# First token quad in four pieces of 32 times, and its fp32 products over nine chunks that stay in memory

## What is computed

```python
x = x + wkv(decay, bonus, layernorm(x), ctx)        # a recurrence over 128 times, per channel
x = x + ffn(layernorm(x), ...)                      # 16 x 128 tokens, D = 512

# wkv, one step: y = (p + E*v) / (q + E);  p, q = decayed p, q plus exp(k)*v, exp(k)
# ffn:
gates = softmax(xf @ gate_w + gate_b)               # top 2 of 16 experts
routed = sum over the 2 experts of gate * (gelu(xf @ ew1 + eb1) @ ew2 + eb2)     # 128 hidden
shared = sum over 2 experts of (gelu(xf @ sw1 + sb1) @ sw2 + sb2)                # 2048 hidden each
```

## Time and profile before

| | |
|---|---|
| Time, median of 3 runs | 881.39 us (880.78 to 884.62) |
| The profiled execution | 879.35 us, of it 877.7 us between its first and last instruction |
| TensorE busy | 844.0 us, 96% |
| VectorE, ScalarE, GpSimd busy | 637.5, 490.8, 185.4 us |
| First instruction of the first split product | 58.85 us |

### The profile page before, as it was taken

One profiled execution on the slowest core, in us unless ns is written; L12 is line 12 of the kernel. 1 busy time (PEld: TensorE's weight loads), 2 busy tenths in 40 slices (PEclk: granted clock), 3 DMA queues, 4 the chain that ended last, 5 costly groups with the idle time before them and its releaser, 6 DMA issues.

```text
span 877.7 us, 14872 instructions
## 1 busy us (share of the span) xinstructions
PE 844.0 (96%) x4054; PEld 700.4 (80%) x4054; DVE 637.5 (73%) x1339; ACT 490.8 (56%) x871; POOL 185.4 (21%) x223
## 2 busy tenths in 40 slices
PE   2599999999999999999999999999999999999997
PEld 2468888888888888888888888888888799897886
DVE  7977988766587778565777786555676698983973
ACT  7737666354476553454656463445455388885531
POOL 2100000121100000122000001110221577764850
PEclk9999999999999999999999999999999999999999
DMA  8353433377343333574433324565687378868985
GB/s 218 97 169 103 139 110 107 105 159 143 93 149 97 97 96 100 125 172 83 157 107 96 97 74 107 119 146 158 179 203 176 113 235 250 256 224 313 307 253 146
DMA packets 124592, 133.37 MB, mean 152 GB/s; under 512 B 10264, under 2 KB 86608, under 8 KB 124012
## 3 DMA queue, kind: packets, MB, share of 16 engines
q1 hardware_dynamic: 115180, 106.90, 44.7%
q0 software_dynamic: 8784, 25.11, 9.5%
q10 hardware_dynamic: 560, 0.55, 0.2%
HBM read 109.53 MB, written 22.98 MB: 151 GB/s over the span
## 4 chain that ended last, share of the span: by engine, by line
PE 94%; DVE 3%; issue 1%; POOL 1%; ACT 0%; DMA 0%; POOLq 0%; ACTq 0%; DVEq 0%
PE up L600 13%; PE up L602 13%; PE up L601 13%; PE acc L662 13%; PE acc L667 13%; PE acc L664 13%; PE up L854 2%; PE up L856 2%; PE acc L600 2%; PE up L763 1%; PE acc L602 1%; PE acc L601 1%; PE misc L627 1%; PE up L627 1%; PE acc L772 1%
## 5 line engine op out<-in xcount | busy, mean ns | idle before, releaser
L600 PE MATMUL up<-xs,w1hi 128*128 128x512 f32 (+1 forms) x512 | 200.9, 392 | 0.0
L602 PE MATMUL up<-xs,w1lo 128*128 128x512 f32 (+1 forms) x512 | 197.6, 386 | 0.0
L601 PE MATMUL up<-xs,w1hi 128*128 128x512 f32 (+1 forms) x512 | 197.2, 385 | 0.0
L662 PE MATMUL acc<-w2hi,hhi 128*128 128x512 f32 x494 | 192.7, 390 | 0.0
L664 PE MATMUL acc<-w2lo,hhi 128*128 128x512 f32 x494 | 192.3, 389 | 0.0
L925 ACT ACTIVATE hhi<-up,b_col 128x512 fp32r<-128x512 f32 x128 | 87.3, 682 | 157.1 <-PE up L602 124.8
L1181 DVE TENSOR_TENSOR hlo<-hf,hhi 128x512 fp32r<-128x512 f32 x128 | 86.8, 678 | 86.6 <-ACT hf L928 40.7
L667 PE MATMUL acc<-w2hi,hlo 128*128 128x512 f32 x494 | 132.6, 389 | 0.0
L602 PEld LDWEIGHTS up<-xs,w1lo 128*128 128x128 f32 x512 | 96.2, 188 | 20.0
L601 PEld LDWEIGHTS up<-xs,w1hi 128*128 128x128 f32 x512 | 96.3, 188 | 18.8 <-issue 0.2
L600 PEld LDWEIGHTS up<-xs,w1hi 128*128 128x128 f32 x512 | 96.2, 188 | 18.8 <-issue 0.2
(11 more groups left out here) (274 smaller groups left out, 1165.1 us busy)
## 6 DMA issues: line engine op xcount, KB each, us to landing
w_raw<-in_L_ffn_sw SPq DMA_DIRECT2D x266, 256.0 KB, 2.9
expert_rows<-ysb SPq DMA_DIRECT2D x47, 256.0 KB
xn_rows<-kn POOLq DMA_DIRECT2D x16, 256.0 KB, 8.0
e2raw<-in_L_ffn_ew SPq DMA_DIRECT2D x16, 256.0 KB, 5.1
ew_sb<-in_L_ffn_ew SPq DMA_DIRECT2D x16, 256.0 KB
X<-in_x SPq DMA_DIRECT2D x12, 256.0 KB, 8.9
vin<-in_ctx SPq DMA_DIRECT2D x12, 256.0 KB
out<-X SPq DMA_DIRECT2D x12, 256.0 KB, 3.9
```

The costliest lines, as they stand in the source:

```text
L600: nc.tensor.matmul(o, lhs[0], rhs[0], start=start, stop=False)
L601: nc.tensor.matmul(o, lhs[0], rhs[1], start=False, stop=False)
L602: return nc.tensor.matmul(o, lhs[1], rhs[0], start=False, stop=stop)
L662: nc.tensor.matmul(acc[t][:], hh, w2hi[:, slot], start=first and (q > 0 or t >= HT) or again, stop=False)
```

## The change

The first quad is worked on in four pieces of 32 times, one tile each, in place of two of 64; every step of the first stage is done per tile, with its own semaphore counts, and the state of the scans is carried over three joints. `PRE` goes from 5 to 9: nine chunks, kept in memory of their own for the whole stage (`pw_a`, `pw_b`, `pw_c`), are multiplied in fp32 for tile 0 and then for tile 1 (18 steps n, 128 tokens each), so that nine chunks of the main stage are done for half the tokens. The queues of the stage are written anew; part of the work on one table (`boost0`) goes from ScalarE to VectorE (`boost_args`); eight transfers of the values are issued by ScalarE. In the first quad's main stage the loop over tiles is written out. What is computed is the same.

```diff
-    PRE = 5
+    PRE = 9
+    N0 = (TB // 2) * PRE
+    T1 = TT + 1
...
-                for j in range(3):
-                    step(at + j)
-                    tile(0, j)
-            with eng.Fori(1 if q == 0 else 0, TB - 1) as tb:
-                for j in range(3):
-                    step(at + 3 * tb + j, at + j)
-                    tile(tb, j)
+                for tb in range(TB - 1):
+                    for j in range(3):
+                        step(at + 3 * tb + j)
+                        tile(tb, j)
+            else:
+                with eng.Fori(0, TB - 1) as tb:
+                    for j in range(3):
+                        step(at + 3 * tb + j, at + j)
...
+            load_tiles([0])
+            load_tiles([1])
+            load_tiles([2, 3])
+            load_values([2, 3])
+            load_pre(0)
+            load_pre(1)
...
-            for p in range(RING):
-                load_pre_w1(p)
-                load_pre_w2(p)
+            for p in range(2, PRE):
+                load_pre(p)
+            for c in range(RING):
+                load_w1(c, c, chunk_of(c))
+                load_w2(c, c, chunk_of(c))
             load_quad(1)
...
+            key_T(0)
+            value_T(0)
+            key_T(1)
+            for i in range(1, TB):
+                value_T(i)
...
-            for tb in range(HT, TB):
-                key_T(tb)
-            value_T(HT)
+            def pre_up_product(n):
+                i, p = divmod(n, PRE)
+                pe.wait_ge(pw1_in[p], 16)
+                pe.wait_ge(xf_ok, i + 1)
+                need(pe, pre_h, n - 2)
                 for k in range(KC):
-                    last = nc.tensor.matmul(up[slot][:, 0:HQ], w1_raw[:, slot, k],
-                                            xf[:, k], start=k == 0, stop=k == KC - 1)
+                    last = nc.tensor.matmul(up[n % RING][:, 0:P], early_w1(p)[:, P * k:P * k + P], xf[:, k, P * i:P * i + P],
+                                            start=k == 0, stop=k == KC - 1)
                 last.then_inc(pre_up, 1)
 
-            def pre_down_product(p):
-                slot = pre_slot(p)
-                pe.wait_ge(pw2_in[slot], 16 * (p // RING + 1))
-                pe.wait_ge(pre_h, p + 1)
-                for t in range(HT):
-                    last = nc.tensor.matmul(acc[t][:], hf[:, slot, P * t:P * t + P], w2_raw[:, slot],
-                                            start=p == 0, stop=False)
-                last.then_inc(pre_down, 1)
-
-            for tb in range(HT):
-                transpose_x(tb, xn[:, tb], acc[HT + tb])
-            pe.wait_ge(xf_ok, HT)
+            def pre_down_product(n):
+                i, p = divmod(n, PRE)
+                pe.wait_ge(pw2_in[p], 16)
+                pe.wait_ge(pre_h, n + 1)
+                nc.tensor.matmul(acc[i][:], hf[:, n % RING, piece(n)], early_w2(p), start=p == 0, stop=False)\
+                    .then_inc(pre_down, 1)
+
+            pe.wait_ge(ek_ok, HT)
+            pe.wait_ge(v_ok, HT + 1)
             pre_up_product(0)
             pre_up_product(1)
-            pe.wait_ge(wexp.sem, wexp.at(1, "e"))
-            pe.wait_ge(ek_half, 2)
-            for p in range(PRE):
-                if p + 2 < PRE:
-                    pre_up_product(p + 2)
-                if p == PRE - 2:
-                    for tb in range(HT, TB):
-                        transpose_x(tb, xn[:, tb], acc[tb])
-                if p == 1:
-                    for tb in range(HT, TB):
-                        result_T(tb)
-                pre_down_product(p)
+            for n in range(N0):
+                if n == 1:
+                    key_T(3)
+                if n in RESULT_AT:
+                    result_T(RESULT_AT[n])
+                if n in X_AT:
+                    early_x(X_AT[n])
+                if n + 2 < N0:
+                    pre_up_product(n + 2)
+                pre_down_product(n)
...
+            def early_reciprocal(i):
+                act.wait_ge(wkv0.sem, wkv0.at(i, "den"))
+                nc.scalar.activation(part(yy, i), part(den, i), ACT.Ln).then_inc(rec0.sem, 1)
+                act.wait_ge(rec0.sem, rec0.at(i, "ln"))
+                nc.scalar.activation(part(yy, i), part(yy, i), ACT.Exp, scale=-1.0).then_inc(rec0.sem, 1)
...
+            first_keep()
+            first_grow()
+            early_exp(0)
+            first_boost()
+            early_values(0)
+            early_exp(1)
+            early_values(1)
+            for b in range(CB // 2):
+                table_grow(b)
+            early_reciprocal(0)
+            for b in range(CB // 2, CB):
+                table_grow(b)
             act.wait_ge(b1_ps, 1)
             nc.scalar.copy(b1_col[:], misc[:, 0:CH]).then_inc(b1_ok, 1)
+            for i in range(HT, TB):
+                early_values(i)
+            for b in range(CB - 6):
+                table_relu(b)
+            x_full(0)
+            early_exp(2)
+            for n in range(2):
+                pre_gelu(n)
+            for b in range(CB - 6, CB):
+                table_relu(b)
+            early_reciprocal(1)
+            early_exp(3)
+            for n in range(2, 5):
+                pre_gelu(n)
+            x_full(1)
+            for n in range(5, 9):
+                pre_gelu(n)
+            x_hi_again(0)
+            early_reciprocal(2)
+            for n in range(9, 11):
+                pre_gelu(n)
+            x_hi_again(1)
+            pre_gelu(11)
+            act.wait_ge(c_in, 16 * 10)
+            for at in (0, 32, 64):
+                nc.scalar.copy(bias_r[at:at + 32], bias_f[at:at + 32]).then_inc(bias_hi, 1)
+            pre_gelu(12)
+            pre_gelu(13)
+            x_hi(2, 1, 2, x_bank[2])
+            pre_gelu(14)
+            early_reciprocal(3)
             table_boost()
+            for n in range(15, N0):
+                pre_gelu(n)
+                split_w1(n - 15, n - 15)
+            x_hi(3, 1, 3, x_bank[3])
 
...
+            def boost_args():
+                dve.wait_ge(pcon.sem, pcon.at(0, "ramp"))
+                after(tab, 0, "uw")
+                for b in range(KC):
+                    last = V.tensor_scalar(boost0[:, b, 1:], ramp[:, 1:], w_down[:, CB + b:CB + b + 1],
+                                           uw[:, CB + b:CB + b + 1], ALU.mult, ALU.add)
+                last.then_inc(boost_arg, 1)
+                dve.wait_ge(boost_arg, 1)
+                V.tensor_scalar(boost0[:, :, 1:], boost0[:, :, 1:], CAP, None, ALU.min).then_inc(boost_arg, 1)
...
+            early_ln1(0)
             tables()
-            early_ln1(0)
             early_ln1_apply(0)
             early_ln1(1)
+            boost_args()
+            early_ln1_apply(1)
             early_es(0)
             early_h(0)
             early_hv(0)
             early_den(0)
-            early_ln1_apply(1)
+            early_ev(0)
             early_num(0)
             early_result(0)
-            early_es(1)
+            early_ln1(2)
             early_add(0)
             early_ln2(0)
+            early_ln1_apply(2)
+            early_ln2_apply(0)
+            early_es(1)
             early_h(1)
-            early_ln2_apply(0)
             early_hv(1)
             early_den(1)
+            early_ln1(3)
+            early_ev(1)
+            early_ln1_apply(3)
             early_num(1)
             early_result(1)
-            for tb in range(HT):
-                x_lo_again(tb)
+            early_es(2)
             early_add(1)
             early_ln2(1)
+            early_h(2)
+            early_ln2_apply(1)
+            early_hv(2)
+            early_den(2)
+            early_ev(2)
+            early_num(2)
+            early_result(2)
+            early_es(3)
+            early_add(2)
+            early_ln2(2)
+            early_h(3)
+            early_ln2_apply(2)
+            early_hv(3)
+            early_den(3)
+            x_lo_again(0)
+            x_lo_again(1)
+            early_ev(3)
+            early_num(3)
+            x_lo(2, 1, 2, x_bank[2])
+            early_result(3)
             gate_weights()
+            early_add(3)
+            early_ln2(3)
             split_w1(0, 0)
-            early_ln2_apply(1)
-            for tb in range(HT, TB):
-                x_lo(tb, 1, tb, acc[tb])
+            early_ln2_apply(3)
             split_w1(1, 1)
+            x_lo(3, 1, 3, x_bank[3])
             split_w1(2, 2)
             bias_low()
```

More of the change, by code:

```diff
@@ L1029, in _ @@
                               .broadcast_to([CB, GB, 32])).then_inc(uw_in, 16)
[L1030 to L1037 removed]
+            for i in range(HT):
+                for g in range(GB):
+                    act.dma_start(vin[32 * g:32 * g + 32, i], vq[0, g, :, i]).then_inc(v_tile[i], 16)
@@ L1251, in early_ln2_apply, with early_stats @@
-            def early_ln2_apply(h):
-                dve.wait_ge(rstd2, h + 1)
-                dve.wait_ge(kT_ps, HT * (h + 1))
-                for tb in range(HT * h, HT * h + HT):
```

(41 more changed lines are left out.)

461 lines of the change are left out of this document (207 added, 254 removed).

## The result

The changed kernel takes 893.97 us (median of four runs, 891.94 to 895.03) where the kernel before takes 881.84 in the same session: a ratio of 1.013, 95% interval 1.0111 to 1.0148. It is 12.1 us slower, and 893.97 lies outside the range of 878.5 to 891. The profiled span is 892.6 us against 877.7. (The profiled execution before lies 2.5 us under its median, so the spans differ by more than the medians.)

What follows compares the result with a forecast made beforehand. TensorE's queue was taken as the bound, with VectorE's equally long in the first stage. First stage +13.35 less 10.48 in the main stage gave +2.9 us: 882.2 on the profiled execution, 884.3 as median, range 878.5 to 891.

Steps and rivals of the forecast that it cites:

- The waits for the reciprocals: First stage: VectorE waits 3.6, 3.3 and 0.5 us for ScalarE's reciprocals of tiles 1, 2 and 3.
- the halved chunks: Main stage, first quad: each halved chunk saves 2.62 us; four more of them save 10.48 us.
- The walk: Step-by-step timing of the first stage's engine queues; it ends at 72.2 us, 13.35 later than before.
- the clock falls: Rival, 0.25: TensorE's first-stage gaps are each followed by up to 5 us at half speed; S 78.9, time 891.
- S: End of the first stage, at TensorE's first split product; forecast at 72.2 us, 58.85 before.
- U: Start of the first fp32 product on TensorE; forecast at 24.85 us, 37.95 before.
- TensorE never paused in either: Main stage: VectorE, full in stretches with halved chunks, does not hold up TensorE; costed at nothing.
- the main stage gives it back: Rival, 0.06: VectorE falls behind over chunks 15 to 26, the four halved chunks save half; +8, 889 us.
- The weight load: Rival, 0.10: in first-stage 128-column fp32 products, weight loading adds to the product, 13 us more TensorE; S about 78, 890.
- reciprocals in time: Rival, 0.13: VectorE does not wait for reciprocals in the first stage; S 64.8 or a little less, 876.9 us.
- R: First routed down product; the time from it to the end was forecast as before, 177.45 us.
- The drain of the Trainium skill: ScalarE, first stage: 1380 ns per table switch, another 8.3 us for three reciprocals, sum +11; left out.

Runs made afterwards that it cites:

- the dummies: Changed kernel plus dummy fp32 products of 384 columns in TensorE's two early idle stretches (5 and 4 of them); 888.6 us, ratio 1.0079.
- the one with the early load: Changed kernel with the third token quad's load issued at main chunk 14 instead of 26; 890.0 us, ratio 1.0078 to the kernel before.
- the version with the exp moved: Changed kernel, third quad loaded at chunk 14, one Ln/Exp table set, ScalarE's first stage reordered, boost table's exp in main stage, result 2 at step 7; 881.87 us.

## Why the prediction was wrong

The waits for the reciprocals came as walked, and the halved chunks save what was forecast. The prediction failed in two places, both of them costs that the sum put at nothing.

**The walk keeps 2.4 GHz behind TensorE's gaps ("Whether 2.4 GHz survives them no row shows").** The walk had the three gaps within half a microsecond and costed what followed at full speed; that they might end it stood as the rival *the clock falls*, at 0.25. That rival was right in kind: two gaps of three were followed by 1.2 GHz. Its S of 78.9 agrees with 78.32, but partly by chance: it priced the slow stretches at 6.7 us (three of them), and the dummies gave back 3.6 (two). Of the 6.1 us by which S was missed, 3.6 are the clock, 0.65 a later U (25.50 for 24.85), and 1.85 is left with the clock at 1.00, in the kernel with the dummies, and grows there tile by tile: the waits for reciprocals 1, 2 and 3 end 0.3, 0.85 and 1.35 us later after U than walked. The rule of the Trainium skill (TensorE: Matmul & The Clock Gate, Part 1) that an idle array drops to half its clock agrees with the rows behind the first two gaps; behind the third, of 2.20 us, the granted clock stayed at 1.00.

**"TensorE never paused in either, so I cost this at nothing."** For the main stage I looked at VectorE and TensorE in the stretches of halved chunks and not at the queue of transfers behind them. The term itself was exact, 10.48 against 10.9 once nothing stops it. But the change moved the chunks against the other transfers, and the weights behind `load_quad(2)` came late: 5.8 us in the profile, 4 on the medians. The rival *the main stage gives it back* had the size (half of the 10.48) and the wrong engine: not VectorE's work but late weights held TensorE up. What remains argued only is what makes the phase bad. In 211:214 the changed kernel's DMA share is 1.46 and the one with the early load has 0.95, and the transfers of weights land five times as late (18.8 for 3.8 us), but which transfers met there I did not separate.

The other steps:
- The weight load does not add: an up product of 128 columns takes 1.05 at full clock and the next starts 0.89 later, where 0.96 was taken and about 1.7 would have come by the rival.
- The reciprocals come late by 3.62, 4.18 and 1.89 us, where 3.6, 3.3 and 0.5 were walked; at full clock they are 3.61, 3.25 and 0.56, so the excess is the clock's. The rival *reciprocals in time* needed them gone; with ScalarE's queue reordered they are (but for 1.16 us at reciprocal 3), and the time is the kernel before's, 881.87, not 876.9: S comes down to 68.1, not 64.8, and what follows R was no shorter.
- A table load is 1.28 us and nothing more: it ends at 33.32 and the logarithm starts at 33.33. The drain of the Trainium skill (ScalarE: Activation LUTs, What ACT_TABLE_LOAD costs), by which the sum would have been +11, is not in the trace. That the total came near that figure is chance.

The sum by measured terms: S +19.5, halved chunks -10.9, the stop +5.8, R to the end +0.5, is +14.9, the difference of the spans.

What stays open: R to the end takes 177.5 to 183.3 us in single executions of these kernels, and runs of one and the same kernel spread as much (876.8 to 884.6 in the version with the exp moved). So gains of 1.5 us in S do not show in the total, and no version is shown to beat the kernel before. A cost behind R that comes with the change is not excluded either: R to the end is 177.5 to 178.3 in the three profiles of the kernel before and its edits, and 180.7 to 183.3 in seven of the ten of the changed kernel and its edits. The version with the exp moved reaches R at 698.59, 1.7 us before the kernel before does (700.25), and loses that behind it.

## What to carry to other kernels

Cutting work into pieces multiplies its fixed round trips. Count the table loads and waits per piece, and place an operation that other engines wait for by when its input is ready. A gap on TensorE can cost more than its length, since the work behind it may run at half speed; a cheap test is to fill the gap with products that nobody reads. When an edit shifts a stage in time, look at the large transfers behind it: they may now fall ahead of something that has no slack.

## What was unexpected in the hardware

- Length alone does not say whether a gap on TensorE costs the clock. After gaps of 2.25, 2.53, 2.71, 2.76, 3.78, 3.84, 4.23 and 5.05 us in these kernels the granted clock fell below 1.00; after 1.95, 2.20 and 2.43 it did not, nor after another of 2.71 (before 54.95, with seven chunks), which is followed by

```profile
54.00:57.00 3.00, 2.05 (x14) 1.77 (x15) 2.78 (x5) 1.57 (x6) 0.00 (x0) 1.00 0.00 0
57.00:60.00 3.00, 2.85 (x18) 1.85 (x17) 2.44 (x8) 2.12 (x5) 1.56 (x2) 1.00 0.00 0
```

- Behind a gelu, a logarithm and an exponential side by side cost two table loads (32.04 and 33.98 in the changed kernel) unless a set that holds both is asked for. Where the program had loaded that set and no gelu had come between, the same pair has none (15.22 and 15.87, reciprocal 0 of the same kernel).
- VectorE's reciprocal of 128x512 takes 3.34 us, its products 0.69.
- Two megabytes of loads, the same in size and number, cost 4.0 to 4.3 us or nothing by where they stand in the queue.
